# Residual sums of two node stages: from identity products on TensorE to additions on GpSimd, with rings of eight tiles

## The reference

```python
edge_index = jnp.stack([src, dst])
x = _layernorm(x + _L0_gnn_ref(x, edge_index, Wl1, Wr1, att1, b1, Wl2, Wr2, att2, b2))
x = _layernorm(x + _L1_gnn_ref(x, W, a, src, dst))
```

## Time and profile before

| | |
|---|---|
| median of 3 runs | 5272.19 us (5264.99 to 5278.1) |
| span of the profiled execution | 5270.5 us |
| PE busy | 3942.9 us (75%) |
| DVE busy | 3296.7 us (63%) |
| POOL busy | 2645.7 us (50%) |
| ACT busy | 1199.0 us (23%) |
| mean granted TensorE clock | 0.887 |

### The profile page before, as it was taken

The page is one execution under the profiler, slowest core; times in us unless marked ns, Lnnn a source line. Parts: engine busy times, 40 slices in busy tenths (PEclk is TensorE's granted clock), DMA queues, the critical chain, the costliest instruction groups (busy, mean ns, idle before and its releaser), DMA issues. The chain is left out here.

```text
span 5270.5 us, 122213 instructions
## 1 busy us (share of the span) xinstructions
PE 3942.9 (75%) x31349; PEld 2833.8 (54%) x31350; DVE 3296.7 (63%) x9997; ACT 1199.0 (23%) x4200; POOL 2645.7 (50%) x2941
## 2 busy tenths in 40 slices
PE   6588878888878795888887888787566666666666
PEld 5355555565655574555555556555344444444443
DVE  6466666666666762666666666666466666666666
ACT  3322222222222362222222222223100000000002
POOL 4455555555555224555555555543455555555550
PEclk8799999999899997999999999989777777777779
DMA  3333333333333123333333333325444434343333
GB/s 91 97 95 98 96 98 95 97 93 93 96 96 99 50 66 88 98 94 99 95 98 92 100 94 98 94 77 156 118 110 109 110 106 112 108 111 108 108 106 104
DMA packets 333905, 521.10 MB, mean 99 GB/s; under 512 B 152887, under 2 KB 219617, under 8 KB 333809
## 3 DMA queue, kind: packets, MB, share of 16 engines
q0 software_dynamic: 120320, 338.39, 23.8%
q1 hardware_dynamic: 213489, 181.58, 12.1%
HBM read 484.14 MB, written 35.46 MB: 99 GB/s over the span
## 5 line engine op out<-in xcount | busy, mean ns | idle before, releaser
L692 POOL DMA_INDIRECT gathered<-table,idx x2496 | 2452.7, 983 | 2090.4 <-POOLq L358 1516.7
L1130 PE MATMUL pS<-gathered,Dm 128*128 128x264 f32 x4992 | 1860.0, 456 | 193.2 <-issue 63.0
L1527 DVE TENSOR_TENSOR acc_mem<-acc_mem,pS 128x264 f32 x2496 | 1048.2, 420 | 466.8 <-remote 224.2
L1069 PE MATMUL pZ<-DT,x 128*128 128x128 bf16 x9984 | 1206.0, 229 | 167.1 <-ACT reluT L864 99.3
L1069 PEld LDWEIGHTS pZ<-DT,x 128*128 x9984 | 926.6, 102 | 598.2 <-issue 341.3
L864 ACT ACTIVATE reluT<-pZ 128x256 f32<-128x256 f32 x1664 | 610.2, 382 | 1990.8 <-PE pZ L1075 1248.1
L1130 PEld LDWEIGHTS pS<-gathered,Dm 128*128 128x128 f32 x4992 | 876.0, 218 | 324.5 <-issue 146.8
L1075 PE MATMUL pZ<-ident,gathered 128*128 128x128 f32 x3328 | 972.5, 292 | 18.0 <-issue 10.7
L1558 DVE TENSOR_TENSOR gathered<-gathered 128x256 f32<-128x256 f32 x2496 | 945.8, 419 | 60.6 <-ACT gathered L856 28.8
L1083 PE MATMUL pL<-reluT,attpad 128*32 128x128 f32 x6656 | 277.5, 286 | 408.4 <-ACT reluT L864 373.3
L1540 DVE TENSOR_TENSOR Dm<-pS,rel_items 128x256 f32<-128x256 f32 x1239 | 515.0, 416 | 0.0
(11 more groups left out here) (232 smaller groups left out, 3335.0 us busy)
## 6 DMA issues: line engine op xcount, KB each, us to landing
DT<-rel_dram SPq DMA_DIRECT2D x156, 512.0 KB
gathered<-table,idx POOLq DMA_INDIRECT x2496
flags<-flag_dram SPq DMA_DIRECT2D x1664, 8.0 KB
span_row<-flag_dram SPq DMA_DIRECT2D x1664, 0.1 KB
table<-xls SPq DMA_DIRECT2D x147, 132.0 KB
flags<-flag_dram SPq DMA_DIRECT2D x416, 32.0 KB
gathered<-table SPq DMA_DIRECT2D x98, 132.0 KB, 2.1
gathered<-in_x SPq DMA_DIRECT2D x98, 128.0 KB, 2.1
```

Source lines behind the costliest of these rows:

```text
L692: nc.gpsimd.indirect_dma_start(out=G[:, b, i, :], out_offset=None, in_=tab[l], in_offset=bass.IndirectOffsetOnAxis(ap=idx[:, b, i:i + 1], ...
L1069: mm = nc.tensor.matmul(z_slot(i)[:, half], x3[:, bass.ds(tk[i], 1), s, half].rearrange("p o c -> p (o c)"), moving, start=(s == 0), stop= ...
L1130: nc.tensor.matmul(pS[:, i % 4, 0:ROW], Dm[:, i % 8, :], G[:, at[0], at[1], :], start=True, stop=True).then_inc(seg_done, 1)
L1527: link(v.tensor_tensor(acc_at(n), acc_at(n), pS[:, n % 4, 0:ROW], ALU.add))
```

## The change

- The residual sum moves to GpSimd: `residual` adds `res` to `tmp` in SBUF, one tile at a time. In stage 2 GpSimd's list is `residual` lag 0, then `clear` lag 0; stage 3 gets a list of its own on GpSimd.
- The bias is added by VectorE in `merged_two`, as a fourth operation. `bias_rows`, the three bf16 rows and TensorE's `residual` and `total` go. TensorE has no part in stage 3 any more.
- `stats` and `normal` read `tmp` (SBUF) in place of `pSum` (PSUM).
- `res`, `tmp` and `small` have eight buffers, `own` and `hbuf` stay at four. Lags: VectorE `finish` 6, `stats` 4; ScalarE `normal` 6, `root` 4, `products` 7, `turned` 6; SyncE in stage 2 `store` 12, `keep` 11, in stage 3 `store` 14.
- `merged_two` now waits for `h_ready`, that is, for ScalarE's `normal` of the tile whose `tmp` it overwrites, in place of `sum_ready`. The load of the own row waits for `acc_read`, that of the residual row for `sum_ready`.

```diff
-        res = in_g(4, D)
-        tmp = in_g(4, D)
+        res = in_g(8, D)
+        xr, r1, zs, ex = (res[:, 2 * n:2 * n + 2, :] for n in range(4))
+        tmp = in_g(8, D)
...
+                    if l == 2 and not (static(t) and t < 4):
+                        sp.wait_ge(acc_read, t + ((l - 1) * TILES - 3))
...
                     if l in (2, 3):
+                        if not (static(t) and t < 8):
+                            sp.wait_ge(sum_ready, t + ((l - 2) * TILES - 7))
                         sp.dma_start(res[:, b, :], (x if l == 2 else hx_dram)[rows(t), :]).then_inc(res_in[b], 16)
...
-                    tiles(sp, (load, 0), (store, 8), (keep, 6), ring=4)
+                    tiles(sp, (load, 0), (store, 12), (keep, 11), ring=8)
                 elif l == 3:
-                    tiles(sp, (load, 0), (store, 6), ring=4)
+                    tiles(sp, (load, 0), (store, 14), ring=8)
...
+                def residual(t, b, h):
+
+                    pool.wait_ge(res_in[b], (h + (l - 2) * EIGHTH[b] + 1) * 16)
+                    pool.wait_ge(acc_read, t + ((l - 1) * TILES + 1))
+                    nc.gpsimd.tensor_tensor(tmp[:, b, :], tmp[:, b, :], res[:, b, :], ALU.add).then_inc(sum_ready, 1)
...
+                elif l == 2:
+                    tiles(pool, (residual, 0), (clear, 0), ring=8)
                 else:
-                    tiles(pool, (clear, 0))
+                    tiles(pool, (residual, 0), ring=8)
+                    return
...
-                    nc.scalar.activation(hbuf[:, b, :], pSum[b], ACT.Identity, scale=small[:, 3, b, 0:1],
+                    nc.scalar.activation(hbuf[:, b4, :], tmp[:, b, :], ACT.Identity, scale=small[:, 3, b, 0:1],
                                          bias=small[:, 3, b, 1:2]).then_inc(h_ready, 1)
...
-                    tiles(act, (merge, 0), (normal, 4), (root, 2), (products, 5), (turned, 4), ring=4)
+                    tiles(act, (merge, 0), (normal, 6), (root, 4), (products, 7), (turned, 6), ring=8)
                 else:
-                    tiles(act, (normal, 4), (root, 2), ring=4)
+                    tiles(act, (normal, 6), (root, 4), ring=8)
...
-                    nc.tensor.matmul(pSum[b], ident[:], res[:, b, :], start=(l == 3), stop=False)
...
-                    nc.tensor.matmul(pSum[b], ident[:], tmp[:, b, :], start=False, stop=True).then_inc(sum_ready, 1)
...
-                elif l == 2:
-                    tiles(pe, (products, 5), (turn_h, 4), (residual, 0), (total, 0), ring=4)
                 else:
-                    tiles(pe, (residual, 0), (total, 0), ring=4)
+                    tiles(pe, (products, 1), (turn_h, 0), ring=4)
...
-                    if not (static(t) and t < 4):
-                        dve.wait_ge(sum_ready, t + ((l - 2) * TILES - 4 + n))
+                    if not (static(t) and t < 8):
+                        dve.wait_ge(h_ready, t + ((l - 1) * TILES - 8 + n))
...
-                        v.tensor_tensor(tmp[:, of, :], tmp[:, of, :], own[:, of, 0:D], ALU.add).then_inc(acc_read, n)
+                        v.tensor_tensor(tmp[:, of, :], tmp[:, of, :], rows, ALU.add).then_inc(bias_step, n)
+                        dve.wait_ge(bias_step, t + n)
+                        v.tensor_tensor(tmp[:, of, :], tmp[:, of, :], bias[:].unsqueeze(1).to_broadcast([P, n, D]), ALU.add).then_inc(acc_read, n)
...
-                    v.bn_stats(small[:, 0, b, 0:6], pSum[b]).then_inc(stat_step, 1)
+                    v.bn_stats(small[:, 0, b, 0:6], tmp[:, b, :]).then_inc(stat_step, 1)
...
-                    tiles(dve, (finish, 4), (merged_two, 0), (stats, 2), ring=4)
+                    tiles(dve, (finish, 6), (merged_two, 0), (stats, 4), ring=8)
...
-                            if l == 1 and s == 7:
-                                bias_rows()
```

More of the change, by code:

```diff
@@ L104, in gnn_program @@
         spare = DT[:, 0, :]
-        wtmp1, b_rest = spare[:, 0:2 * D].bitcast(F32), spare[:, 4 * D:6 * D].bitcast(F32)
-        b_high, b_mid, bias3, ones_bf = (spare[:, o:o + n] for o, n in ((2 * D, D), (3 * D, D), (6 * D, D), (7 * D, P)))
+        wtmp1 = spare[:, 0:2 * D].bitcast(F32)
         Dm = sb("Dm", [P, 8, P])
@@ L221, in gnn_program @@
         own_in = [sem(f"own_in{b}") for b in range(4)]
-        res_in = [sem(f"res_in{b}") for b in range(4)]
+        res_in = [sem(f"res_in{b}") for b in range(8)]
         h_ready = sem("h_ready")
@@ L361, in gnn_program @@
         QUARTER = [(TILES + 3 - b) // 4 for b in range(4)]
+        EIGHTH = [(TILES + 7 - b) // 8 for b in range(8)]
         def tiles(eng, *parts, ring=2, apart=0):
@@ L476, in node_loads @@
             def node_loads(l, *more):
-                ring = 4 if l > 1 else 2
                 def load(t, b, h):
-                    if not (static(t) and t < ring):
+                    if l < 2 and not (static(t) and t < 2):
                         if l == 0:
                             sp.wait_ge(h_turned, t - 1)
-                        elif l == 1:
+                        else:
                             sp.wait_ge(acc_read, t - 1)
-                        else:
-                            sp.wait_ge(sum_ready, t + ((l - 2) * TILES - 3))
+                    if l == 2 and not (static(t) and t < 4):
+                        sp.wait_ge(acc_read, t + ((l - 1) * TILES - 3))
                     if l == 0:
@@ L499, in store @@
                         if static(t) and t == TILES - 1:
-                            sp.dma_start(out[t * P:N, :], hbuf[0:LAST, b, :]).then_inc(out_stored[b], 16)
+                            sp.dma_start(out[t * P:N, :], hbuf[0:LAST, b % 4, :]).then_inc(out_stored[b % 4], 16)
                         else:
-                            sp.dma_start(out[rows(t), :], hbuf[:, b, :]).then_inc(out_stored[b], 16)
+                            sp.dma_start(out[rows(t), :], hbuf[:, b % 4, :]).then_inc(out_stored[b % 4], 16)
                         return
@@ L663, in node_pool @@
                     tiles(pool, (later_low, 2), (later_rest, 1), apart=8)
-                else:
-                    tiles(pool, (clear, 0))
+                elif l == 1:
+                    tiles(pool, (clear, 0))
+                elif l == 2:
+                    tiles(pool, (residual, 0), (clear, 0), ring=8)
+                else:
+                    tiles(pool, (residual, 0), ring=8)
+                    return
                 pool.wait_ge(mm_done, (l + 1) * TILES)
@@ L1348, in merged_two @@
                     else:
+                        b4, h4 = by_four(b, h)
                         for k in range(n):
-                            dve.wait_ge(own_in[b + k], (h + (HALF[b + k] if b + k < 2 else 0) + 1) * 16)
-                        mine = by_head(own[:, of, 0:D])
+                            dve.wait_ge(own_in[b4 + k], (h4 + (HALF[b4 + k] if b4 + k < 2 else 0) + 1) * 16)
+                        rows = own[:, b4:b4 + n, 0:D]
+                        mine = by_head(rows)
                         v.tensor_tensor(mine, mine, spread_heads(wx), ALU.mult)
@@ L1381, in stats @@
                     dve.wait_ge(sum_ready, t + ((l - 2) * TILES + 1))
-                    if not (static(t) and t < 4):
-                        dve.wait_ge(h_ready, t + ((l - 1) * TILES - 3))
-                    v.bn_stats(small[:, 0, b, 0:6], pSum[b]).then_inc(stat_step, 1)
+                    if not (static(t) and t < 8):
+                        dve.wait_ge(h_ready, t + ((l - 1) * TILES - 7))
+                    v.bn_stats(small[:, 0, b, 0:6], tmp[:, b, :]).then_inc(stat_step, 1)
                     dve.wait_ge(stat_step, 1)
@@ L1651 @@
 W_IN = [48, 112, 192]
-W_STEPS = [6, 12, 27]
+W_STEPS = [6, 12, 20]
 EARLY = 4
```

44 lines of the change are left out of this document (13 added, 31 removed).

## The result

The kernel after has a median of 5303.15 us (13 runs, 5293.62 to 5322.34), the kernel before, run beside it, 5278.1 (13 runs, 5264.99 to 5293.74): a ratio of 1.0037, 95% interval 1.0024 to 1.0051 (the two medians alone give 1.0047). It is slower by about what was forecast, and lies in the range. The profiled execution has a span of 5291.8 us against 5270.5: +21.3, where the sum said +23.2.

The account below looks back on a forecast made before the run. Stage 2 was taken as bound by a loop of VectorE, ScalarE, SyncE and DMA, TensorE beside it. 18.4 + 8.8 - 1.5 - 0.3 - 3.5 + 1.3 = +23.2 us on 5270.5: 5293.7, 5295 as a run; range 5274 to 5312.

Parts of the forecast that it names:

- `bias_rows`: Ahead of stage 2: its removal takes VectorE's work there away, -3.5 us (bounds 0 and -4.5).
- fill: Stage 2, start to third root: later merges and statistics 5.2 us, GpSimd's blocking the rest, +8.8 (bounds +5 and +12).
- twenty pairs: Stage 2, third to 23rd root: pairs of 6.3 us for 5.38, +18.4; short last merge and less GpSimd work, -1.5.
- drain: Stage 2, 23rd root to last copy: seven tiles at 2.01 us a tile, 14.3 us against 14.54, -0.3.
- stage 3: Pairs keep their 3.22 us; later statistics and GpSimd against the denominators in the fill, +1.3 (bounds 0 and +4).
- What bounds the kernel before: Stage 2: a loop VectorE, ScalarE, SyncE, DMA sets 5.38 us a pair, 0.8 of it waiting for the own row.
- Load wait gone, bias in its place: Stage 2 merge: load wait of 0.8 us a pair goes, bias as fourth operation costs 0.79; pair 5.35.
- The wait for `normal`: Stage 2: the merge waits for ScalarE's `normal`, 1.44 us behind the root, not 1.10; pair 5.69.
- Blocking by GpSimd: Stage 2: GpSimd's zeros hold up the merge's first two operations, 0.6 us a pair (bounds nothing and about 1.3).
- TensorE's clock: Stage 2, a rival: at the low clock two tiles, 2 x (2.01 + 1.1) us, just fit into 6.3; chance 0.15.
- rival (c): Stage 2: TensorE's granted clock falls, costing the drain 7 us and perhaps 2 more, 5304; chance 0.15.
- Edges 2: The edge stage between stage 2 and stage 3: no change in length, 0 us.

Follow-up runs that it names:

- e5: Kernel before, with SyncE's stage 2 lags changed: store 10 for 8, keep 8 for 6. Ratio 1.0053, stage 2 177.14 us.
- e11: Kernel before, with VectorE's list in both node stages reordered to merge, finish, statistics. Ratio 1.0034, stage 2 172.25 us, stage 3 82.49 us.
- e2: Kernel after, with two idle float32 products a tile added on TensorE in stage 2. Pair 6.19 us, stage 2 169.30 us against 175.98.
- e8: e2 without VectorE's addition of the bias in stage 2. Pair 5.40 us, stage 2 151.24 us.
- e4: Kernel after without VectorE's addition of the bias in stage 2. Pair 6.41 us, stage 2 173.73 us.
- e7: e2 with GpSimd's two zero-writing operations cut to one column. Pair 6.04 us, stage 2 165.53 us.
- e6: e2 with VectorE's wait for `normal` moved behind the merge's first operation. Pair 5.89 us, stage 2 163.00 us.
- e9: Kernel after, with ScalarE's lag for `products` in stage 2 at 8 in place of 7. Pair 6.23 us, stage 2 174.83 us.
- e1: Kernel after, with GpSimd's two zero-writing operations in stage 2 cut to one column. Pair 6.41 us, stage 2 175.99 us against 175.98.
- e3: Kernel after, with VectorE's wait for `normal` in stage 2 moved behind the merge's first operation. Pair 6.37 us, stage 2 175.43 us.
- e10: e9 with VectorE's merge put ahead of `finish` in both node stages. Ratio 1.0081, pairs 6.92 and 3.99 us.
- e12: e10 with ScalarE's `root` lag at 5 in place of 4 in both node stages. Ratio 1.0041, stage 2 179.91 us, stage 3 85.20 us.

## Why the prediction came out

The time and the sign were right. The path to them was right in most steps and wrong in one that hid itself. Part of the hit is luck: five terms miss the table by -1.0 (`bias_rows`), -2.5 (fill), +1.0 (twenty pairs), +2.9 (drain) and -2.3 us (stage 3), and these sum to -1.9.

- **What bounds the kernel before**: right in kind; SyncE's list is in the loop (e5, e11). Its 0.8 us a pair no run shows alone.
- **Load wait gone, bias in its place**: right. No DMA wait is left at the merge in the middle, and the bias costs 0.79 of a pair where VectorE's loop is the bound (e2 to e8), and nothing at the low clock (e4).
- **The wait for `normal`**: right in kind, low in size. It was taken as 1.44 us from root to merge; e2 has 0.79 + 0.61 and then 0.38 to the merge, 1.78. The 0.06 allowed for the signal should have been some 0.35. The gap is there with the zeros of one column too: 0.34 in e7 (`normal` ends at 3652.15, the merge starts at 3652.49).
- **Blocking by GpSimd**: the mechanism right, 0.6 a pair wrong: 0.15 (e7, for the zeros). The room between GpSimd's last operation and the merge was worked out from a wait of 1.44, and it is 1.78. Where the merge does come early (e6), VectorE's operations are 0.35 to 0.6 longer. These two errors nearly cancel, by luck: VectorE's loop was put at 6.3, and is 6.19.
- **TensorE's clock**: this is the step that failed, and the reading of the kernel after rests on it. The prediction held it a rival of 0.15, and said that two tiles at the low clock "just fit" into 6.3. The clock did fall, to 0.50, for nearly all of the stage. A tile of that loop is 3.20, not 2.01 + 1.1 = 3.11: the products are 1.00 longer, and from their modelled end to ScalarE's copy it is 0.22 at the low clock (3655.91 behind 3653.51 + 2.18) where it is 0.04 at the full one (3740.56 behind 3739.34 + 1.18, rows below). That does not fit into 6.3 but sets 6.41. Of the 0.99 us that a pair grew by, VectorE's loop explains 0.77 and the clock the last 0.22 (e2, e9). By the prediction's view, less work of GpSimd or of VectorE in a pair would have helped; at this clock neither helps (e1, e3, e4).
- **Fill**: +6.3 against +8.8; the bound below was 5. The blocking was there as said, but smaller: to the next operation the second merge takes 3.62 us, 0.8 more than free (1.4 forecast), the denominators 7.32, 1.2 more than before (1.5), and the third pair's merge 0.16 more (0.6). The zeros alone are 0.9 us of the fill: in e1, with one column of them, the third root stands at 32.42. The first merge starts 0.35 nearer to the stage's start. Some 0.9 of the miss stays open. VectorE in the fill of the kernel after (0.68, 0.69 and, by the like-shaped L1292, 0.43 when free), then ScalarE and TensorE in its drain:

```profile
3575.64 1.21 DVE L1342 TENSOR_TENSOR gathered<-acc_mem,gathered 128x512 f32<-128x512 f32 x1
3576.95 0.97 DVE L1344 TENSOR_TENSOR gathered<-gathered 128x512 f32<-128x512 f32 x1
3580.64 0.86 DVE L1293 TENSOR_TENSOR gathered<-gathered 128x180 f32<-128x180 f32 x1
...
3740.56 0.18 ACT L791 ACTIVATE Dm<-pS 128x8 f32<-128x8 f32 x1 [0.79 <-PE pS L976]
...
3739.34 1.18 PE L976 MATMUL pS<-W,gathered 128*128 128x272 f32 x4 [0.60 <-ACT gathered L775]
```

- **Twenty pairs**: +17.9 against 18.4 - 1.5 = 16.9.
- **Drain**: +2.6 against -0.3, the low clock again: in e2, at full clock, it is 14.32, as forecast. TensorE is granted full clock only for the last tiles of it (0.69 in 3720 to 3740); rival (c) named this cost and put it at 7.
- **`bias_rows`**: the edges end 4.5 us earlier; 3.5 forecast. VectorE's operations, counted back from the end of the edges, tell which part is its own. The addition (L1527 before, L1518 after) ahead of `bias_rows` starts at 3540.09 and 3538.82, 1.27 us earlier already; the first behind it at 3545.60 and 3541.31, 4.29 earlier. So 3.0 us came with `bias_rows`, where VectorE now waits 0.60 for TensorE; the 1.27 came before it, and its cause stays open.
- **Stage 3**: pairs of 3.22 right; the whole 1.0 us shorter, 1.3 longer forecast, outside its bounds of 0 to 4. This is not scatter: stage 3 takes 88.55 to 88.72 us in e1 to e4 and e6 to e9, 89.65 in e5. Up to the third root it grew by 0.65 only; from the third to the 23rd it is 1.1 shorter (63.54 against 64.61), with early pairs of 2.85 to 2.91; behind that 0.5 is gained, about the 0.6 of the prediction. So the fill was put 1.2 too high, and the shorter early pairs were not foreseen.
- **Edges 2**: as long as before, as the prediction took it. Only its first gather comes 3.0 us earlier behind the last copy (3.96 against 7.00); VectorE's L1478 did not move with it.

## What to carry over

Taking work off an engine that is not the bound can still slow the stage, where its granted clock falls and a chain through it grows (here 3.20 us a tile for 2.01): work out the chain at the low clock first, and compare it with the pace you forecast. When two loops lie within some per cent of each other, an edit to one shows nothing; lift the other (here, by idle products) before you judge a part. And before a lag or an order in one engine's list is changed, go through every ring that the list feeds: in e5, e10 and e12 a wait that was to go came back as another or stayed.

## What the runs showed of the hardware

- In both kernels TensorE's first products with the weights in stage 2 ran at the 1.2 GHz level, 2.18 us for four. Ahead of the transposes that feed them TensorE had been idle for 7 us before, for 26 after. Before, the granted clock was 1.00 from 3600 us on; after, it stayed at 0.50 to 0.59 up to 3720, though the engine was busy 16.44 of 20 us there (3700 to 3720). In e2 it was 1.00 in a stretch with 13.98 of 20 us busy. A busy share read from the page does not tell which level it was done at, nor whether the clock will rise.
- The mutual blocking of VectorE and GpSimd catches even operations of two columns (L1390: 0.60 for 0.17), and such an operation can stand in a chain, as in e12.
- From the end of ScalarE's `normal` to the VectorE operation that waits for it, 0.34 to 0.38 us pass. Where the wait stands last before the operation (e3) it is 0.18; with two more waits behind it in VectorE's list, 0.34 or more. Whether those waits are the reason was not tried.
